# A decoder layer on one core: the feed-forward's first rows, signs and scales are made inside the attention stage, and its first three blocks of hidden units follow the last output projection

## What is computed

```python
x = x + mamba(layernorm(x), ...)
x = x + xattn(ctx, ctx, layernorm(x), mask, ...)
x = x + ffn(layernorm(x), w1, b1, w2, b2)

def binarize(w):                          # value: mean|w| per row, times sign(w)
    return mean(abs(w), axis=1, keepdims=True) * sign(w)

def ffn(x, w1, b1, w2, b2):               # w1 is 2048 x 512, w2 is 512 x 2048
    h = gelu(einsum('bsd,hd->bsh', x, binarize(w1)) + b1, approximate=False)
    return einsum('bsh,dh->bsd', h, binarize(w2)) + b2

def xattn(v, k, q, mask, ...):            # per head, 32 wide
    attn = softmax(qh @ kh.T / sqrt(32) + mask * -1e9)
    return (attn @ vh).reshape(...) @ Wo + bo
```

## Time and profile before

| | |
|---|---|
| median of 3 runs | 3619.19 us (3605.59 to 3627.15) |
| the profiled execution | 3605.01 us, its span 3603.7 us |
| mean granted clock of TensorE | 0.957 |
| busy: PE, DVE, ACT, POOL | 3227.3, 2657.5, 2388.7, 1791.1 us |
| attention: 14 sequences' periods, first to last | 1021.93 us |

### The profile page before, as it was taken

One profiled execution on the slowest core, in us unless ns is written; L12 is line 12 of the kernel. 1 busy time (PEld: TensorE's weight loads), 2 busy tenths in 40 slices (PEclk: granted clock), 3 DMA queues, 4 the chain that ended last, 5 costly groups with the idle time before them and its releaser, 6 DMA issues. The chain is left out here.

```text
span 3603.7 us, 59690 instructions
## 1 busy us (share of the span) xinstructions
PE 3227.3 (90%) x20864; PEld 2268.9 (63%) x20864; DVE 2657.5 (74%) x4676; ACT 2388.7 (66%) x5306; POOL 1791.1 (50%) x1133
## 2 busy tenths in 40 slices
PE   5789988989889998999997999999999999689998
PEld 4556655666556665666554666666666666478787
DVE  2899999999999999999984676667767776422221
ACT  5777788777887778877853676666666666432222
POOL 2778888888888888888871000000000000045454
PEclk8899999999999999999998999999999999899999
DMA  5566666666657666666662131112111211211010
GB/s 169 163 174 194 189 170 158 175 194 188 169 157 185 184 187 172 161 181 179 178 184 94 33 105 46 46 51 79 51 46 52 83 47 46 59 39 35 24 47 24
DMA packets 286153, 425.02 MB, mean 118 GB/s; under 512 B 28609, under 2 KB 225985, under 8 KB 281250
## 3 DMA queue, kind: packets, MB, share of 16 engines
q1 hardware_dynamic: 272781, 407.22, 40.4%
q10 hardware_dynamic: 13077, 13.99, 1.3%
HBM read 320.12 MB, written 101.02 MB: 117 GB/s over the span
## 5 line engine op out<-in xcount | busy, mean ns | idle before, releaser
L798 POOL TENSOR_TENSOR a_hs<-a_rep,a_bmat 128x896 f32<-128x896 f32 x512 | 1061.5, 2096 | 277.1 <-PE a_yps L310 277.0
L430 ACT ACTIVATE a_states<-a_rep,a_a_neg 128x224 f32<-128x224 f32 x2048 | 795.8, 439 | 80.5 <-DVE a_hs L694 78.9
L687 DVE TENSOR_TENSOR_SCAN a_states<-a_states,a_hs 128x900 f32<-128x900 f32 x384 | 780.0, 2031 | 80.4 <-ACT a_states L430 65.2
L1334 DVE CUSTOM_DVE_ANT_0 b_sc<-b_sps,early_mask 112x375 f32<-112x375 f32 x1024 | 500.2, 546 | 151.2 <-PE b_sps L1131 151.0
L1147 PEld LDWEIGHTS b_tps<-ident,b_sc 112*125 112x125 f32 x3072 | 403.8, 192 | 290.4 <-issue 170.7
L1147 PE MATMUL b_tps<-ident,b_sc 112*125 112x112 f32 x3072 | 491.5, 290 | 82.7 <-DVE b_pT L1348 40.5
L1242 ACT ACTIVATE b_sc<-b_sc,b_nmax 112x750 f32<-112x750 f32 x512 | 468.0, 915 | 62.6 <-DVE b_nmax L1340 62.6
L1426 POOL TENSOR_SCALAR early_var_eps<-early_mv 112x2 f32<-112x2 f32 x15 | 3.2, 215 | 946.7 <-DVE early_mv L1303 946.7
L332 PE MATMUL a_work<-early_scan_hT,w_in 128*128 128x224 f32 x2048 | 424.1, 362 | 6.4 <-issue 3.9
L694 DVE TENSOR_TENSOR a_hs<-a_states,a_cmat 128x896 f32<-128x896 f32 x384 | 419.2, 1092 | 13.2
L332 PEld LDWEIGHTS a_work<-early_scan_hT,w_in 128*128 128x128 f32 x2048 | 395.2, 195 | 48.7 <-issue 42.0
(11 more groups left out here) (169 smaller groups left out, 5080.4 us busy)
## 6 DMA issues: line engine op xcount, KB each, us to landing
a_rep<-du_scratch SPq DMA_DIRECT2D x512, 224.0 KB, 5.6
w_in<-W_in_dram SPq DMA_DIRECT2D x128, 512.0 KB, 4.3
du_scratch<-early_du SPq DMA_DIRECT2D x16, 1792.0 KB, 11.3
ctx<-ctxT_dram SPq DMA_DIRECT2D x48, 500.0 KB, 6.0
v_scratch<-kv_out SPq DMA_DIRECT2D x96, 250.0 KB
k_scratch<-kv_out SPq DMA_DIRECT2D x96, 250.0 KB, 4.5
b_keys<-k_scratch SPq DMA_DIRECT2D x8, 1500.0 KB, 11.5
b_v<-v_scratch SPq DMA_DIRECT2D x8, 1500.0 KB
```

What stands on the lines that cost most here:

```text
L430: e = act.activation(rows(states[:, g % DA, :])[:, q, 1:ROW], rep[tile % REPS][:, j, 0, :], ACT.Exp, scale=a_neg[:, g % SLOTS, q:q + 1])
L687: dve.tensor_tensor_scan(state if g % G4 else whole, state, whole, 0.0, ALU.mult, ALU.add).then_inc(S["scan"], 1)
L798: pool.tensor_tensor(hs[g % RING][:, :, 1:ROW], rep[tile % REPS][:, j, 1, :].unsqueeze(1).broadcast_to([P, Q, L]), bmat[b % 2][:], ALU.mul ...
L1334: dve.tensor_tensor_reduce(out=sc[block % 2][:, j, cols], in0=sps[0:TT, j, 0:HALF], in1=mask[:, block % 2, cols], scale=-1.0, scalar=3.0e3 ...
```

## The change

The feed-forward's preparation moves into the attention stage. In the last sequence's slots the first 512 rows are loaded, normalised, transposed and split (`load_rows`, `normalise_rows`, `transpose_rows`, `keep_rows`, `split_rows`), the first quarter of w2 is loaded and its signs made; the scales are made near the beginning of the stage. The inverse standard deviation of `x2`'s rows is no longer made once for all rows in the feed-forward: for each sequence POOL and ACT make it (`rsqrt_of_x2`, `guess_rsqrt_x2`), and `store_stats` stores it in place of the variance. After the last slot PE makes the first three blocks of hidden units (`hidden(0..2)`) into banks that the feed-forward keeps, and ACT loads the table with GELU. The feed-forward then starts with the GELU of block 0; the three later quarters of w2 are loaded by SyncE at its start. Buffers are laid out so that these tiles outlive the stage.

```diff
@@ attention_phase
+        LAST = (B - 1) * SLOTS
+        ROWS_AT = (LAST + 13, LAST + 15, LAST + 16, LAST + 17)
-        slots = range(-6, B * SLOTS + SLOTS // 2 + 1)
+        slots = range(-6, B * SLOTS + SLOTS // 2 + 2)
 tensor_program:
+            def hidden(f):
+                pe.wait_ge(S["s1"], KD)
+                pe.wait_ge(S["rows_lo"], KD)
+                pe.wait_ge(S["ttr"], GROUP * N_ALL)
+                ...
+                mm.then_inc(S["f_ps"], 1)
+                if slot == 8:
+                    spread_alpha()
+                if slot in ROWS_AT:
+                    transpose_rows(ROWS_AT.index(slot))
+            for f in range(3):
+                hidden(f)
+            pe.wait_ge(S["f_ps"], 3)
 scalar_program:
+            def guess_rsqrt_x2(b):
+                act.wait_ge(S["x2_var"], b + 1)
+                act.activation(x2_guess[:], x2_var[:], ACT.Ln).then_inc(S["x2_log"], 1)
+                act.wait_ge(S["x2_log"], b + 1)
+                act.activation(x2_guess[:], x2_guess[:], ACT.Exp, scale=-0.5).then_inc(S["x2_guess"], 1)
+                if slot - LAST - 10 in range(4):
+                    sign_w2(slot - LAST - 10)
+                    if at == SLOTS + 9:
+                        guess_rsqrt_x2(b)            # behind keep_q and keep_sums of the slot
+                if slot in ROWS_AT:
+                    keep_rows(ROWS_AT.index(slot))
+            act.preload_act_table_set("gelu_and_others")
 vector_program:
+                if slot == 6:
+                    scales()
+                if slot == 9:
+                    keep_alpha()
+                if slot == LAST + 11:
+                    normalise_rows()
+                if slot in ROWS_AT:
+                    split_rows(ROWS_AT.index(slot))
 gpsimd_program:
+            def rsqrt_of_x2(b):
+                pool.wait_ge(S["stats"], b + 1)
+                if b:
+                    pool.wait_ge(S["x2_guess"], b)
+                pool.tensor_scalar(x2_var[:], mv2[:, 2 * b:2 * b + 2, 1], EPS, None, ALU.add).then_inc(S["x2_var"], 1)
+                pool.wait_ge(S["x2_guess"], b + 1)
+                pool.wait_ge(S["x2_var"], b + 1)
+                newton_rsqrt(steps, mv2[:, 2 * b:2 * b + 2, 1], x2_guess[:], x2_var[:], x2_tmp[:]).then_inc(S["x2_rstd"], 1)
+                    if at == SLOTS + 8:
+                        rsqrt_of_x2(b)
 sync_program:
             def store_stats(b):
-                sp.wait_ge(S["stats"], b + 1)
+                sp.wait_ge(S["x2_rstd"], b + 1)
                 sp.dma_start(mv_dram[b].rearrange("(i p) c -> p i c", p=TT),
                              mv2[:, 2 * b:2 * b + 2, :]).then_inc(S["stats_out"], 16)
+                if slot == LAST - SLOTS:
+                    load_mv(0, 4, "mv_in0")
+                if slot == LAST + 4:
+                    load_rows()
+                    load_w2()
+                if slot == LAST + 9:
+                    load_mv(4, ready, "mv_in1")
                 for b in range(B):
...
@@ ffn_phase
-        slots = range(-12, STEPS * FT + LAG + 1)
+        slots = range(STEPS * FT + LAG + 1)
+        MADE = 3
 tensor_program:
-            pe.wait_ge(S["weights"], 16 * 2)
-            pe.wait_ge(S["const"], KD + 2)
-            for k in range(KD):
-                mm = pe.matmul(tps[:, k * P:(k + 1) * P], ones[:], diag[:, k, :], start=True, stop=True)
-            mm.then_inc(S["alpha2_ps"], 1)
-            pe.wait_ge(S["alpha2"], 1)
-                if 0 <= slot < ALL:
+                if MADE <= slot < ALL:
                     hidden(slot)
 scalar_program:
-                if slot + 1 in range(0, FT, F // D):
-                    sign_w2((slot + 1) // (F // D))
+                if slot + 1 in range(QUARTER, FT, QUARTER):
+                    sign_w2((slot + 1) // QUARTER)
                 if 0 <= slot < ALL:
                     gelu(slot)
 gpsimd_program, in each slot behind split_g(slot):
-                    if at == -8:
+                    if at == -8 or slot == c == 0:
                         add_b2(c)
 sync_program:
+            for a in range(1, KD):
+                sp.dma_start(w2[a - 1][:], w2T[a]).then_inc(S[f"w2_{a}"], 16)
+            load_mv()
-        act.dma_start(mv[:], ...).then_inc(S["mv_in"], 16)
-        for dst, src in ((b1[:], t["b1"]), (b2[:], t["b2"].partition_broadcast(P))):
-            act.dma_start(dst, src).then_inc(S["weights"], 16)
-        for a in range(KD):
-            act.dma_start(w2[:, quarter[a], :], w2T[a]).then_inc(S[f"w2_{a}"], 16)
-        rstd_of_rows(act, dve_steps, mem, S, mv, rstd)
```

More of the change, by code:

```diff
@@ L982, in mamba_phase, with attention_phase @@
         mem.end()
[L985 to L999, removed]
+def attention_phase(nc, t, x1_dram, x2_dram, k_dram, v_dram, mv_dram, mv2, row_mv, wsum, ident, shared, early, sps):
     B, D, KEYS = t["ctxT"].shape
@@ L1045, in attention_phase @@
         oT = [mem.sbuf(f"oT{i}", [P, GROUPS, L]) for i in range(2)]
-        sps = mem.psum("sps", [P, 4, BANK])
+        x2_var, x2_guess, x2_tmp = (mem.sbuf(name, [TT, 2]) for name in ("x2_var", "x2_guess", "x2_tmp"))
+        alpha2 = mem.sbuf("alpha2", [P, KD])
+        diag = mem.sbuf("diag", [P, KD, P])
+        ones = mem.sbuf("ones", [P, P])
+        last_w2 = mem.arena("last_w2", [P, D])
+        raw_w2 = [*(early[f"raw_w2_{i}"] for i in range(3)), mem.inside("raw_w2_3", [P, D], last_w2)]
+        s2 = [*(early[f"sign_w2_{i}"] for i in range(3)), mem.inside("sign_w2_3", [P, D], last_w2, F32R)]
+        alpha1, alpha2_row, b1, b2 = (early[name] for name in ("alpha1", "alpha2_row", "b1", "b2"))
+        rows_in, rows, rowsT = early["x_0"], early["rows"], (early["rowsT_hi"], early["rowsT_lo"])
+        F = t["w1"].shape[0]
+        FT = F // P
+        T = 4 * P
+        LAST = (B - 1) * SLOTS
+        ROWS_AT = (LAST + 13, LAST + 15, LAST + 16, LAST + 17)
         tps = mem.psum("tps", [P, 2, BANK])
@@ L1505, in attention_phase, with ffn_phase @@
         mem.end()
-def ffn_phase(nc, t, x2_dram, mv_dram, out, wsum, ident, shared, early):
+        return s2
+def ffn_phase(nc, t, x2_dram, mv_dram, out, row_mv, ident, shared, early, first_s2, sps):
     B, L, D = x2_dram.shape
@@ L1523, in ffn_phase @@
         s1 = shared.s1
[L1524 to L1533, removed]
-        xt = [mem.sbuf(f"xt{i}", [P, TILES, D]) for i in range(3)]
-        ln = mem.sbuf("ln", [P, TILES, D])
-        hT = [[mem.sbuf(f"hT{i}_{n}", [P, KD, T], F32R) for n in ("hi", "lo")] for i in range(2)]
+        QUARTER = F // D
+        b1, b2, alpha1, alpha2_row = (early[name] for name in ("b1", "b2", "alpha1", "alpha2_row"))
+        places = [mem.arena(f"w2_{a}", [P, QUARTER, D]) for a in range(1, KD)]
+        w2 = [mem.inside(f"raw_w2_{a}", [P, QUARTER, D], place) for a, place in enumerate(places, 1)]
+        signs = [mem.inside(f"sign_w2_{a}", [P, QUARTER, D], place, F32R) for a, place in enumerate(places, 1)]
+        s2 = [*(tile[:] for tile in first_s2), *(tile[:, i, :] for tile in signs for i in range(QUARTER))]
+        xt = [early[f"x_{i}"] for i in range(3)]
+        ln = early["rows"]
+        hT = [[early["rowsT_hi"], early["rowsT_lo"]], [mem.sbuf(f"hT1_{n}", [P, KD, T], F32R) for n in ("hi", "lo")]]
         g32 = [mem.sbuf(f"g32_{i}", [P, T]) for i in range(2)]
@@ L1604, in tensor_program @@
                     second(slot - LAG)
-                for c in range(STEPS):
+                for c in range(1, STEPS):
                     at = slot - c * FT
@@ L1608, in tensor_program, with loads @@
                         transpose_h(c, at + 6)
+        def loads(c):
+            return c // 3 + (c % 3 > 0)
         def after_second(engine, n):
```

199 lines of the change are left out of this document (132 added, 67 removed).

## The result

The changed kernel takes 3691.21 us (median; 3686.78 to 3693.75), the kernel before 3612.39 us in the runs beside it (3604.39 to 3627.15): ratio 1.0212, 95% interval 1.0173 to 1.0251. It is slower by about 79 us. The forecast was 3670, with a range from 3632 to 3708. Of all executions reported here, one (6324 us, of the kernel with the operations alone) lies far outside the rest and is left out of its ratio.

What follows compares the result with a forecast made beforehand. PE was taken as close to full in all three stages, idle for preparation at the border. Against the profiled 3605.0, border -31, one-time work +6, wait +66 and clock +24 gave +65: 3670, range 3632 to 3708.

Steps and rivals of the forecast that it cites:

- The border: Between attention and feed-forward: preparation leaves PE's path and the second block's products start earlier, a gain of 31 us.
- The wait: SyncE at each sequence's end: store_stats waits for x2_rstd, x1's load starts 4.85 us later; 66 us lost over 14 sequences.
- Its slope: VectorE's wait for x1 in attention: nine tenths of a delay come out as time (1.08 us later cost 0.97).
- the expectation for the kernel before: Storing the statistics behind the loads in the kernel before would bring the time 10 to 25 us below before.
- The clock: PE behind the waits for x1 in attention: clock falls in nearly all sequences, 11 more at 2.2 us, 24 us.
- the 76 to 79 that were named as a sign: Attention's sequence periods: 76 to 79 us would show the forecast right, 71 to 73 with the late store wrong.
- The rival that the clock holds: Attention: the loads of x1 are late but PE's clock doesn't fall, 3646 us; chance 0.18.
- What the attention stage takes in once: Scales, first rows' preparation and signs of one quarter of w2 moved into attention: at most 18.5 us, a third taken, 6.
- the 90: The loss forecast in attention's 14 periods: 66 us for the wait and 24 for the clock.

Runs made afterwards that it cites:

- the kernel with the operations alone: The kernel before plus the per-sequence inverse standard deviation of x2 on POOL and ACT, result unused, store_stats waiting for the plain statistics as before: 3616.67 us, ratio 1.0005.
- the pair of kernels that differ in it alone: The kernel before plus x2's per-sequence rsqrt on POOL and ACT, unused; with store_stats waiting for it 3719.15 us, without that wait 3616.67 us.
- The kernel before without any wait: The kernel before with the store of the statistics met four slots later, behind the loads of x1, keys and values: 3610.81 us, ratio 0.9999.
- the changed kernel without the wait: The changed kernel with the statistics stored four slots later, behind the load of x1, except in the last sequence: 3593.98 us, ratio 0.9952.
- the kernel before with the shift: The kernel before with one unused tile of 224 bytes per partition ahead of the stretch that stages share, moving all addresses behind it: 3619.45 us, ratio 1.0017.

## Why the prediction was right, and where it was not

**The border** was right to a fraction of a microsecond, -30.8 for -31, and by its own steps: blocks behind the last projection, first GELU 9 us after it, POOL's b2 and split as what sets the second block's products. The signs of the second quarter of w2 waited 2.19 us for their load on ACT without holding PE up.

**The wait** was sized from one sequence: 4.85 us forecast, 4.77 measured; idle time ahead of L1366 up by 67.8 us, 66 forecast. That this wait and nothing else is the loss is shown by the pair of kernels that differ in it alone, 3719 and 3617.

Its slope was read wrongly, though. Nine tenths of a delay came from two sequences, of which the first lay on the floor. The trace of before has more periods at the full clock, such as these, with waits of 0.69 and 0.99 us:

```profile
2642.23:2713.57 71.34, 65.88 (x588) 45.28 (x584) 50.50 (x180) 48.73 (x109) 3.51 (x7) 1.00 0.18 58
...
2856.92:2928.56 71.64, 65.79 (x588) 45.21 (x584) 50.50 (x180) 48.73 (x109) 3.52 (x7) 1.00 0.20 57
```

With 71.19 for a wait of 0.43 and 72.16 for 1.50 they show a floor of 71.2 us, about half a microsecond that is free, and beyond it a slope of one. The kernel before without any wait has the same floor and the same time. So a delay is free until the slack is used up, and from there costs its whole length, and the clock's falls on top; as the delay here was about ten times the slack of half a microsecond, the sum hardly felt the mistake. At a small delay the same step would have promised a gain that isn't there, and did, in the expectation for the kernel before.

**The clock** was forecast at 24 us, by 11 more falls of 2.2. It fell in all 14. By the periods, 97.6 - 67.8 = 29.8 us lie beside the waits if the comparison is with the kernel before. If it is with the changed kernel without the wait, the half microsecond of slack comes off each of the 14 waits: 96.3 - (79.5 - 7) = 24. That this meets the forecast is in part luck: the falls counted are 14, not 11 more, and where no load is awaited single periods with falls lie 1.6 to 4.7 us over the floor (72.9 to 76.0 against 71.3). The periods after, 78.3 to 84.6 us, came out over the 76 to 79 that were named as a sign. The split can't be had closer, because the clock also falls in some sequences without a wait. Of "TensorE: Matmul & The Clock Gate" (Trainium skill) the section on HAM oscillation says that a transfer awaited with each tile brings the clock down with each tile; here it did, 14 times in 14 at 4.8 us of delay and 12 in 14 at 1.9. The rival that the clock holds is out.

**What the attention stage takes in once** was over-sized: 1.2 us (-0.8 and +2.0), for 6.

**What was missing** is the pace of the feed-forward's matmuls, 6.5 us, of which a shift of addresses alone makes 5.1. The prediction put nothing for it: it took their durations as given, since no instruction of them changes, but the diff moves their operands all the same. 11.3 us more lie in the Mamba stage, in which the change alters nothing but addresses. Four profiles of kernels with the Mamba stage of before end it between 1936.59 and 1948.25 us, and the kernel before with the shift at 1944.08, so one profile can't give this a cause; the profile of before has the lowest of them. The profiled execution of before lies 7 us below the median beside it, the one after at its median; so the spans differ by 85.9 us and the medians by 79, and against the medians the forecast is 14 us short.

The sum, term by term: +10.5 ahead of the 14 periods (Mamba's 11.3 and the -0.8), +7.6 in them beyond the 90, -4.0 in the last sequence, +0.2 at the border, +6.5 behind it: 20.8 of the 20.9 us between +65 and +85.9.

## What to carry to other kernels

A store that waits holds up every transfer behind it in the same engine's list: before a store is made to wait for one more result, look at what the list issues next, and put the store behind the loads that somebody waits for. That one move turned a loss of 2.1% into a gain of 0.5%. A slope of time against delay, read from two sequences of which one lies on the floor, holds neither below the slack nor above it; and a new small tile ahead of others moves their start addresses, so the pace of instructions that a diff doesn't touch is worth one look at the profile after.

## What the runs showed of the hardware

- 8 fp32r matmuls that stream 512 columns take 1.81 to 1.82 us at 2.4 GHz where, by the kernels' lists of tiles, the streamed tile and the weights start alike within 256 bytes, and 1.86 to 1.87 where one starts at a multiple of 256 and the other 224 bytes past one (in the changed kernel also 192 past against 0): 5 to 6 us of 426 in this feed-forward. That it is the offset between the two, and not the one start or the other, fits all these kernels but wasn't tested by itself, and why wasn't tried. "SBUF — State Buffer" (Trainium skill), in its section on operand start alignment, states only which starts are legal and says that its runs timed nothing.
- In the kernel with Ln and Exp ahead of keep_q, TensorE kept 2.4 GHz behind idle times of VectorE of 1.04 and 1.24 us; behind twelve of 2.21 to 3.17 us there, and fourteen of about 5.7 in the changed kernel, it fell to 1.2 GHz for a while. The length of the wait doesn't decide it alone: in the kernel before, the clock held behind a wait of 1.50 us and fell behind one of 0.81 (the sequence from 2206.14, whose mean granted clock is 0.98) as well as behind the one of 1.56. It fell as well in some sequences that waited for no load, which stays unexplained.
